# Attention and GRU kernel: the transposes of a tile's q and k, their copy and the second projection at other places of the slot

## The reference, cut to what matters

```python
# x: (4, 512, 512), cond: (4, 512), float32, 16 heads of 32
scale, shift = split(cond @ W_emb + b_emb)
xn  = rms_norm(x, g_norm) * (1 + scale) + shift
q, k, v = split(xn @ W_qkv)                # each (512, 16 heads, 32) per batch
q, k = rms_norm(q, g_q), rms_norm(k, g_k)  # over the 32 values of a head
attn = softmax(q @ k.T * 32 ** -0.5)       # (512, 512) per head
o    = attn @ v
x    = x + o + o @ W_out
x    = x + GRU(initial_state=cond, inputs=x)   # 512 steps, batch 4, state 512
```

## Time and profile before

| what | us |
|---|---|
| three runs, median (lowest to highest) | 2194.8 (2192.48 to 2197.61) |
| the profiled execution, its own time | 2185.68 |
| the profiled execution, span from first to last instruction | 2183.8 |
| start of the first slot with scores (slot 6) | 33.29 |
| start of slot 64, the first without a projection | 501.87 |

### The profile page before, as it was taken

One profiled execution on the slowest core, in us unless ns is written; L12 is line 12 of the kernel. 1 busy time (PEld: TensorE's weight loads), 2 busy tenths in 40 slices (PEclk: granted clock), 3 DMA queues, 4 the chain that ended last, 5 costly groups with the idle time before them and its releaser, 6 DMA issues.

```text
span 2183.8 us, 129719 instructions
## 1 busy us (share of the span) xinstructions
PE 2121.6 (97%) x58385; PEld 1693.5 (78%) x58385; DVE 1246.5 (57%) x4456; ACT 1121.3 (51%) x4603; POOL 198.6 (9%) x225
## 2 busy tenths in 40 slices
PE   8999999999899999999999999999999999999997
PEld 5665666655688888888888888888888888888776
DVE  4765656657355555555555555555555555555554
ACT  5775766656244444444444444444444444444444
POOL 4442433322100000000000000000000000000000
PEclk9999999999999999999999999999999999999999
DMA  6000000001100001000000000010100000010000
GB/s 220 1 21 1 2 20 2 2 1 59 39 20 22 23 20 30 17 27 19 28 18 26 22 25 26 17 31 16 30 16 28 18 29 19 25 29 18 23 5 13
DMA packets 42439, 54.90 MB, mean 25 GB/s; under 512 B 8064, under 2 KB 35740, under 8 KB 41884
## 3 DMA queue, kind: packets, MB, share of 16 engines
q1 hardware_dynamic: 41012, 43.40, 6.3%
q0 software_dynamic: 528, 3.15, 0.4%
q10 hardware_dynamic: 344, 0.05, 0.0%
HBM read 29.80 MB, written 16.78 MB: 21 GB/s over the span
## 4 chain that ended last, share of the span: by engine, by line
PE 90%; DVE 4%; ACT 3%; issue 2%; DMA 1%; POOL 1%; SPq 0%; POOLq 0%; ACTq 0%; DVEq 0%
PE ps L526 58%; PE ps L428 7%; PE ps L512 7%; PE ps L334 7%; PE ps L449 3%; PE ps L465 3%; PE ps L396 3%; DVE znT L874 2%; DVE xb L885 1%; ACT z_trip L709 1%; ACT xb L712 1%; DMA x1T<-in_L_cond_W_emb 0%; POOL qk_rs L311 0%; PE ps L550 0%; DMA seeds<-gi_spill 0%
## 5 line engine op out<-in xcount | busy, mean ns | idle before, releaser
L526 PE MATMUL ps<-wqkv,xb 128*4 128x128 f32 x49152 | 1462.2, 273 | 35.8 <-DVE xb L885 27.3
L526 PEld LDWEIGHTS ps<-wqkv,xb 128*4 128x4 f32 x49152 | 1221.3, 87 | 255.1 <-DVE xb L885 149.0
L709 ACT ACTIVATE z_trip<-znT 128x8 f32<-128x8 f32 x1024 | 219.4, 214 | 365.1 <-DVE znT L874 365.1
L885 DVE TENSOR_TENSOR_SCAN xb<-z_trip,xb 128x24 f32<-128x24 f32 x1024 | 213.4, 208 | 259.9 <-ACT xb L712 259.9
L890 DVE STREAM_TRANSPOSE rT<-ps 128x128 f32<-128x128 f32 x512 | 162.4, 317 | 344.9 <-PE ps L526 344.9
L874 DVE STREAM_TRANSPOSE znT<-ps 128x128 f32<-128x128 f32 x1024 | 313.2, 306 | 64.6 <-PE ps L526 4.0
L703 ACT ACTIVATE r_pair<-rT 128x16 f32<-128x16 f32 x512 | 111.9, 219 | 434.2 <-DVE rT L890 434.2
L512 PE MATMUL ps<-wih,x1T 128*32 128x256 f32 (+1 forms) x4096 | 236.2, 326 | 0.0
L879 DVE TENSOR_TENSOR_SCAN ps<-r_pair,znT 128x16 f32<-128x16 f32 x1024 | 204.5, 200 | 36.1 <-DVE znT L874 1.4
L712 ACT ACTIVATE xb<-ps 128x16 f32<-128x16 f32 x1024 | 190.8, 186 | 21.5 <-DVE ps L879 1.3
L428 PE MATMUL ps<-wqkv,xnT 128*128 128x384 f32 x512 | 200.5, 498 | 1.0 <-ACT xnT L617 1.0
(11 more groups left out here) (75 smaller groups left out, 969.6 us busy)
## 6 DMA issues: line engine op xcount, KB each, us to landing
gi_spill<-gi_image SPq DMA_DIRECT2D x64, 192.0 KB, 2.1
seeds<-gi_spill SPq DMA_DIRECT2D x228, 32.0 KB
seeds<-gi_spill SPq DMA_DIRECT2D x284, 16.0 KB
out<-xb SPq DMA_DIRECT2D x60, 64.0 KB
wih<-in_L_cond_W_ih SPq DMA_DIRECT2D x1, 3072.0 KB, 14.6
xb<-in_x SPq DMA_DIRECT2D x3, 1024.0 KB, 5.8
wqkv<-in_L_cond_W_hh POOLq DMA_DIRECT2D x1, 3072.0 KB, 10.8
wqkv<-in_L_cond_W_qkv SPq DMA_DIRECT2D x3, 768.0 KB, 9.3
```

The costliest lines, as they stand in the source:

```text
L526: last = nc.tensor.matmul(ps[QD * j:QD * j + B, bank, 0:P], hist_flat[:, first:first + 3 * B - 2:3], weights, start=False, stop=False, ski ...
L709: nc.scalar.activation(z_trip[:, 8 * half:8 * half + 8, 2], znT[:, half, 0:16:2], ACT.Sigmoid).then_inc(s[z_name], 1)
L885: return nc.vector.tensor_tensor_scan(next_elements(step, half), z_trip[:].rearrange("p e s -> p (e s)")[:, 24 * half:24 * half + 24], ele ...
```

## The change

The transposes of q and k go behind the values, `project(1)` goes from behind pt1 to behind pt0, and on ScalarE the copy of the transposed q and k goes from ahead of the first exponential to behind it. Nothing is added or removed. In slots up to 5, which have no quad, nothing changes.

```diff
--- before.py
+++ after.py
@@ -451,8 +451,6 @@
                         if hh == 0 and i >= ALL_TILES:
                             transpose_rexp()
 
-                if slot >= LAG and i < ALL_TILES:
-                    transpose_qk(i)
                 if 0 <= m - 1 < ALL_QUADS:
 
                     g, q = divmod(m - 1, TT)
@@ -467,6 +465,8 @@
                                 v_sb[:, g % G, kc, QD * hh:QD * hh + QD], probsT[:, hh, kc, :],
                                 start=(kc == 0), stop=(kc == TT - 1), tile_position=(0, QD * hh))
                     last.then_inc(s["pv_done"], 1)
+                if slot >= LAG and i < ALL_TILES:
+                    transpose_qk(i)
 
                 if n < ALL_TILES:
                     if n == TT:
@@ -487,7 +487,7 @@
                         for kc in range(TT):
                             last = transpose(ps[:, SC[hh], P * kc:P * kc + P], probs[:, hh, P * kc:P * kc + P])
                         last.then_inc(s["pt_done"], 1)
-                    if n < ALL_TILES and hh == 1:
+                    if n < ALL_TILES and hh == 0:
                         project(1)
                 if n < ALL_TILES:
                     project(2)
@@ -663,10 +663,10 @@
                     act.wait_ge(s["rtr_done"], m)
                     nc.scalar.activation(rT_sb[:, g % 2, P * q:P * q + P], ps[:, PJ[slot % 2], 3 * P:4 * P],
                                          ACT.Copy).then_inc(s["r_ready"], 1)
-                if slot >= LAG and i < ALL_TILES:
-                    evacuate_qk(i)
                 if 0 <= m < ALL_QUADS:
                     for hh in range(4):
+                        if hh == 1 and i < ALL_TILES:
+                            evacuate_qk(i)
                         act.wait_ge(s["max_done"], 4 * m + hh + 1)
                         nc.scalar.activation(probs[:, hh, :], ps[:, SC[hh], :], ACT.Exp,
                                              bias=negmax[:, m % 2, hh:hh + 1],
```

## The result

The changed kernel takes **2189.5 us** (median of 10 runs, 2184.0 to 2193.1), the kernel before 2195.2 in the same comparison: a ratio of 0.9975, 95% interval 0.9964 to 0.9987. That is 5.7 us less, between 2.9 and 7.9; 2187.6 was predicted. Beside the experiments the same kernel was timed again: 2188.4 us (12 runs), ratio 0.9965, interval 0.9951 to 0.9980.

The account below looks back on a forecast made before the run. TensorE's own sequence was taken to bound the kernel. Savings of 4.6 (46 plain slots), 2.0, 1.0 and 0.1, less 0.2 and 0.3, gave 7.2 us: 2194.8 to 2187.6 us, range 2182 to 2194.

Parts of the forecast that it names:

- TensorE's saving of 0.19 per slot: Plain slots: with transposes behind the values, 0.09 on the second transpose and 0.10 on `project(0)` go, giving 6.90.
- Scores to values costs nothing more: TensorE, scores directly followed by values: extra handover cost taken as 0, the values' entry being in their 1.01.
- The upper bound of 0.24: Most that scores to values might cost: the longest delay ahead of the q and k transposes that a row shows.
- the third rival: ScalarE's copy waits for late transposes and holds up exponentials 1 to 3; at worst 0.24 per slot, 2201.3 us; chance 0.09.
- The rule on weight loads: TensorE: by it joining whole-array work hides no load, giving the second rival's 2192.5 us; the prediction held the trace against it.
- The copy between exponentials at 0.28: ScalarE: the copy behind the first exponential makes exponentials 1 to 3 come 0.28 later; its whole duration is 0.38.
- The 0.51: Rival on ScalarE: step between copy and exponential 0.51, not 0.28, adding 13.1 for 2200.7 us; chance 0.03.
- pt3 late, 0.09 given back: TensorE's last transposes: wanted at 5.17, fourth exponential seen at 5.19; 0.02 late plus entry 0.06, taken as 0.09; slot 6.99.
- `project(1)` as cover: TensorE: behind pt0 the projection costs 0 and covers exponential 1, which is 0.28 late.
- Odd slots: Six slots gain 0.33 each, three 0.36, slot 6 about 0.1; 8 and 9 lose about 0.1 each, 64 loses 0.3.
- The difference of 9.1 between profile and median: Median of runs stands 9.1 above the profiled time, taken as outside this stage and carried over to the forecast.
- the one in which the exponentials hide: Rival: pt3 isn't late and the full 0.19 per plain slot is kept, 12.6 less, 2182.2 us; chance 0.10.

Follow-up runs that it names:

- one handover more: Transposes of q and k moved into the middle of the values (behind 16 of 32 matmuls), against the changed kernel: 2198.0 us, ratio 1.0019 to the kernel before.

## Why the prediction was right

- *TensorE's saving of 0.19 per slot:* right. The pair of transposes and `project(0)` each fell by 0.10 by the rows (0.09 said for the pair), and the kernel with the copy behind the fourth exponential, where nothing is late, takes 6.89 where 6.90 was worked out.
- *Scores to values costs nothing more:* right, 1.07 and 1.01 as kept. This was the step without a row. The first step inside the values is 0.133 behind the scores as it was behind the transposes, so this is a handover too, with the same small price on the way in. The upper bound of 0.24 was not one of a handover: the earlier trace rows is slot 12, where the transposes wait for VectorE's copy of a piece. It weighed only in the third rival's worst case.
- *The rule on weight loads,* taken from the Trainium skill ("TensorE: Matmul & The Clock Gate", Part 3, The mechanism), that a weight load overlaps matmuls in flight only when its row group differs: right to doubt. By it the slot would have stayed at 7.09, and the kernel with one handover more at 6.99; they take 6.99 and 7.22. The same section of the Trainium skill also lets a load be pulled ahead when it goes to the background weight buffer, which the prediction left out; with that case the trace is not at odds.
- *The copy between exponentials at 0.28:* right (0.27 in the rows), and the kernel in which it alone moves excludes 0.38 and 0.51. The 0.51 came from the Trainium skill ("ScalarE: Activation LUTs", Rules for kernel authors), whose 0.3 us is for an activation with its bias as a pointer operand. The copy has no such operand, so the page's 0.51 was not one for this copy. The transposes reach the copy just in time. The sum had 0.01 between the two, less than the rows can resolve, so that no wait at all came of it is in part luck.
- *pt3 late, 0.09 given back:* right, 1.40 instead of 1.31, and taken away by moving the copy. pt3 is late by 0.04 and not 0.02, with 0.05 for the late start; the 0.01 put on for rounding covered most of that. The slot of 6.99 is exact, to the hundredth by some luck.
- *`project(1)` as cover:* right, 0.18 a slot.
- *Odd slots:* slot 12's kind gave 0.36 (0.33 said), slot 27's 0.36 each as said. Slots 8 and 9 lose 0.03 and not 0.1; in slot 9 the first exponential, bound by ScalarE's late work of the slot before, comes 2.25 after the start instead of 2.29. **Slot 65 was wrong:** I called it even. It has 0.37 more (5.61 to 5.98): its transposes come 2.67 after its start, the copy waits for them, and behind it three exponentials, which is the third rival in one slot. Its copy on ScalarE and pt1 to pt3 on TensorE:

```profile
502.90 0.38 ACT L655 ACTIVATE qkT<-ps 128x256 f32<-128x256 f32 x1 [0.28 <-PE ps L334]
504.01 1.99 PE L334 MATMUL ps<-ident,probs 128*128 128x128 f32 x12 [0.68 <-ACT probs L671]
```

The kernel in which only the copy moves keeps slot 65 at 5.59, and the one with the copy behind the third exponential at 5.58: it takes both, late transposes and a copy early in the row.
- *The sum:* 7.2 said, 7.3 to 7.4 in the traces. The two medians say 5.7 and 8.4, and the 7.4 lies inside both intervals. That it comes so close is partly that misses cancel: slot 65 costs 0.4 that wasn't counted, and slots 6, 8, 9, 64 and the nine that used to wait came out 0.5 better together than said.
- *The difference of 9.1 between profile and median,* carried over: right to carry, and its cause is in the main known. The profiled execution of before had a short GRU.

Of the rivals, the one in which the exponentials hide needs another place of the copy. There the stage is 14.9 us shorter (482.9 against 497.7), 12.6 said. The plain slots give 9.0 of it (8.7 said); the slots of another kind give more (0.48 for slot 12's kind where 0.42 was said, 0.63 for slot 27's where 0.45 was said, and 1.1 in slots 6, 8, 9, 64 and 65, which that sum left out).

## What to carry to other kernels

Count the changes between whole-array and tiled work on TensorE and put whole-array pieces side by side; here the first and last steps beside a change cost 0.12 us together on the way from transposes to values, 0.17 from values to transposes and 0.22 from values to a projection. When a small copy leaves idle time for a place in a busy chain, ask which instruction behind it is wanted first, and look for the next gap: behind the last exponential it was free, ahead of the second or the fourth it cost half the gain. And judge such a change by the stage's length in the trace when the rest of the kernel scatters by more than the gain.

## What the runs showed of the hardware that was not expected

The GRU stage, the same code in every kernel, took 1593 us in one execution and 1599 to 1607 in the thirteen other traces. What differs is a wait that no other engine ends, ahead of TensorE's weight loads. The waits of the first trace of before, from 600 to 2150 us (total, times, longest):

```profile
PEld ps L526 <- issue: 3.6, 13, 0.5
```

and of the changed kernel:

```profile
PEld ps L526 <- issue: 14.0, 42, 0.6
```

The second trace of before has 13.5 in 45 waits. Over the traces the GRU is on the whole the longer the more of such waits it has: 10.0 us with a GRU of 1599.2 (one handover more), 15.2 with one of 1606.9 (the changed kernel again). So most of the 14 us between the first trace of before and that of the changed kernel goes with TensorE's weight loads being late now and then where no other engine holds them up. That it is also the 9 us between that profile and the median is likely, but the runs without a trace can't show it. What makes the loads late wasn't tried; it stays open.
